# Second layer's attention: far score blocks made transposed by the matmul itself, four heads of a group per unit

## The reference, cut to what matters

```python
q = (x @ Wq.T) ... * hd ** -0.5        # 16 heads
k, v = ...                             # 4 groups, each repeated for 4 heads
scores = einsum('bhqd,bhkd->bhqk', q, k)
dist = clip(pos[None, :] - pos[:, None], -127, 127) + 127
bias = einsum('bhqd,kqd->bhqk', q, E[dist])
attn = softmax(scores + bias, axis=-1)
out = einsum('bhqk,bhkd->bhqd', attn, v) ... @ Wo.T
```

## Time and profile before

| | us |
|---|---|
| median of 3 runs | 1951.91 (1949.84 to 1952.54) |
| profiled execution, its own time | 1956.96 |
| its span in the trace | 1954.9 |

### The profile page before, as it was taken

How to read it: one execution, slowest core, us unless ns; L and a number is a source line. 1 busy time by engine, 2 the same in 40 slices (tenths; PEclk the granted TensorE clock), 3 DMA queues, 4 the chain that set the end, 5 groups by cost and what they waited for, 6 DMA issues and landing times. The chain is left out here.

```text
span 1954.9 us, 48846 instructions
## 1 busy us (share of the span) xinstructions
PE 1600.0 (82%) x17207; PEld 1157.0 (59%) x17207; DVE 1109.7 (57%) x3204; ACT 919.3 (47%) x1570; POOL 829.4 (42%) x1346
## 2 busy tenths in 40 slices
PE   3799999969999996326993269999995799999945
PEld 2466667655666664315762247777774577777733
DVE  5566666574666666560332756566566566565652
ACT  2355555444555553000321157777773466666622
POOL 2255555423555552024353025555552255555500
PEclk9899999989999998557997579999997799999968
DMA  3000000000000000421342025555550355555400
GB/s 116 1 1 0 0 0 0 1 1 1 1 0 0 0 0 1 167 94 56 76 94 39 5 92 183 179 177 179 180 172 1 115 180 179 179 176 180 152 1 22
DMA packets 102707, 146.63 MB, mean 75 GB/s; under 512 B 11632, under 2 KB 59120, under 8 KB 102640
## 3 DMA queue, kind: packets, MB, share of 16 engines
q1 hardware_dynamic: 95856, 140.87, 23.0%
q0 software_dynamic: 6784, 4.87, 1.9%
HBM read 68.49 MB, written 77.21 MB: 75 GB/s over the span
## 5 line engine op out<-in xcount | busy, mean ns | idle before, releaser
L496 ACT ACTIVATE t_Pt<-t_psT 128x512 f32<-128x512 f32 x1024 | 556.5, 595 | 471.2 <-PE t_psT L385 471.2
L468 POOL TENSOR_SCALAR t_Z<-t_Z,t_m 128x1024 f32<-128x1024 f32 x512 | 574.3, 1122 | 0.0
L385 PE MATMUL t_psT<-idf,t_Z 128*128 128x128 f32 x4096 | 562.2, 281 | 14.6 <-POOL t_Z L468 13.4
L385 PEld LDWEIGHTS t_psT<-idf,t_Z 128*128 128x128 f32 x4096 | 454.9, 145 | 100.7 <-ACT t_Pt L496 47.0
L439 DVE CUSTOM_DVE_ANT_0 t_Z<-t_psS,a1b_A 128x1024 f32<-128x1024 f32 x256 | 312.4, 1220 | 201.0 <-issue 201.0
L439 DVE CUSTOM_DVE_ANT_0 t_Z<-t_psS,a0b_L 128x1024 f32<-128x1024 f32 x256 | 312.3, 1220 | 190.0 <-issue 187.3
L360 PE MATMUL t_psO<-t_Pt,t_Vh 128*32 128x128 f32 x8192 | 329.9, 279 | 0.0
L467 POOL TENSOR_TENSOR t_touch<-t_m 128x1 f32<-128x1 f32 x512 | 98.7, 193 | 490.9 <-DVE t_m L439 488.9
L360 PEld LDWEIGHTS t_psO<-t_Pt,t_Vh 128*32 128x32 f32 x8192 | 192.4, 109 | 191.0 <-ACT t_Pt L496 158.1
L488 ACT ACTIVATE t_rows<-t_psE 128x512 f32<-128x512 f32 x256 | 152.9, 597 | 16.4 <-PE t_psE L346 15.3
L337 PE MATMUL t_psS<-a0b_KT,a0b_QT 72*128 (+1 forms) x512 | 154.7, 383 | 6.7 <-PEq L74 4.1
(11 more groups left out here) (233 smaller groups left out, 1444.5 us busy)
## 6 DMA issues: line engine op xcount, KB each, us to landing
relative_rows<-t_rows SPq DMA_DIRECT2D x256, 256.0 KB, 2.0
a1b_A<-relative_rows SPq DMA_DIRECT2D x192, 192.0 KB, 2.5
a1b_A<-relative_rows SPq DMA_DIRECT2D x64, 128.0 KB, 2.2
x_B<-in_b SPq DMA_DIRECT2D x1, 4096.0 KB, 18.1
x_A<-in_a SPq DMA_DIRECT2D x1, 4096.0 KB, 25.5
expert_rows<-zp SPq DMA_DIRECT2D x1, 2740.0 KB, 11.6
x_xe<-expert_rows SPq DMA_DIRECT2D x8, 342.5 KB, 3.1
x_WP<-in_moe_pre SPq DMA_DIRECT2D x8, 256.0 KB, 3.2
```

The source lines that it names most:

```text
L385: last = nc.tensor.transpose(psT[:, half, k * P:(k + 1) * P], Z[:, qt % 2, kt * P:(kt + 1) * P], idf[:])
L468: nc.gpsimd.tensor_scalar(Z[:, qt % 2, :], Z[:, qt % 2, :], -1.0, m[:, qt % 2:qt % 2 + 1], ALU.mult, ALU.add).then_inc(s_sub, 1)
L496: nc.scalar.activation(Pt[:, qt % 2, half * (N // 2):(half + 1) * (N // 2)], psT[:, half, :], ACT.Exp).then_inc(s_exp, 1)
```

## The change

The first layer keeps `attend`. The second layer uses a new function `attend_direct`, the clearing of A goes, and `project` scales the queries by plus instead of minus. The unit of work is now a group G: the four heads of one key/value group for one query tile; there are 32 groups per batch entry, all written out in code (no hardware loop). For each group and each key block kt one item of 128 keys x (4 heads x 128 queries) is made in a psT slot (a ring of three), exponentiated and multiplied with V:

- Scores with queries on the partitions are still made for all keys (`scores`, in chunks of 512 keys in a ring of three PSUM banks), but DVE writes out only the band (sum with A into Zb, with its maximum) and takes a plain `reduce_max` over the rest; `group_max` joins the parts.
- POOL subtracts the maximum from the band (four instructions of up to 384 elements) and splits the negated maximum into three bf16 parts (six small instructions on 128 x 4).
- PE turns these parts (`turn_max`) to 12 rows, DVE copies them out of PSUM (`max_rows`), and SP moves them by three DMAs into rows 72 to 74 of QT, against three rows of ones in KT. With them one bf16 matmul of 75 rows by 512 columns makes the scores of a far item already transposed and less the maximum.
- Band items are transposed as before, four per item.
- `values` runs per item, one head in each column strip; the eight items of a group are summed in PSUM, so one `to_rows` and one copy and division serve four query tiles of four heads.

```diff
+def attend_direct(nc, tag, b, QT, KT, V, attn, con, segments, EBT, scratch):
...
+    def item(G, i):
+        return G * 9 + (i if i < 4 else i + 1)
...
+                def ring_free(n):
...
+                    before = n - RR
+                    G, pos = before // 9, before % 9
+                    if pos == 4:
+                        if G + 1 < GROUPS:
+                            pe.wait_ge(s_me, G + 2)
+                        if G % 4 == 1 and G > 4:
+                            pe.wait_ge(s_div, G // 4)
+                    else:
+                        pe.wait_ge(s_exp, G * 8 + (pos if pos < 4 else pos - 1) + 1)
...
+                def unit(G, i):
...
+                    if kt in band(qt):
+                        if i == 0:
+                            pe.wait_ge(s_sub, (G + 1) * J)
+                        for j in range(J):
+                            last = nc.tensor.transpose(out[:, j * P:(j + 1) * P], Zb[...], idf[:])
+                    else:
+                        if kt == off(qt)[0]:
+                            pe.wait_ge(s_md[G % 2], 48 * (G // 2 + 1))
+                        var = 1 if kt * P < lo(qt) else 2
+                        last = nc.tensor.matmul(out, KT[0:KM, var * GKV + hq, kt * P:(kt + 1) * P],
+                                                QT[0:KM, hq * J:(hq + 1) * J, qt * P:(qt + 1) * P], start=True, stop=True)
+                    last.then_inc(s_u, 1)
...
+                for G in range(-3, GROUPS):          # PE
+                    for i in range(QT_N):
+                        if G >= 0:
+                            unit(G, i)
+                        if i < 2:
+                            if G >= 1:
+                                values(G - 1, i + 6)
+                        elif i == 2:
+                            if G >= 0 and (G == 0 or G % GRP):
+                                values(G, 0)
+                        elif i == 3:
+                            if G >= 0:
+                                if G and G % GRP == 0:
+                                    values(G, 0)
+                                values(G, 1)
+                        elif G >= 0:
+                            values(G, i - 2)
+                        if 0 <= G + 2 < GROUPS:
+                            scores(G + 2, i // 2, i % 2)
+                        if i % 2 and G + 3 < GROUPS:
+                            relative(G + 3, i // 2)
+                        if i == 3 and G >= 0:
+                            n = G * 9 + 4
+                            ring_free(n)
+                            if G + 1 < GROUPS:
+                                turn_max(G + 1, n)
+                            if G % 4 == 1 and G > 4:
+                                to_rows(G // 4 - 1, n)
...
+                for G in range(-2, GROUPS):          # DVE
+                    for j in range(J):
+                        if G + 2 < GROUPS:
+                            tile(G + 2, j)
+                            if j == J - 1:
+                                group_max(G + 2)
+                        if j == 0 and G > 0 and G % GRP == 0:
+                            copy_out(G // GRP - 1)
+                        if j == 2:
+                            if 0 <= G and G + 1 < GROUPS:
+                                max_rows(G + 1)
+                            if G % 4 == 1 and G > 4:
+                                divide(G // 4 - 1, G * 9 + 4)
...
+                            if i % 2 and G + 3 < GROUPS:      # ACT, after the exponential of item i
+                                gather(G + 3, i // 2)
...
+                def max_rows(G):                     # SP
+                    hq, qt = G // QT_N, G % QT_N
+                    sp.wait_ge(s_me, G + 1)
+                    for s in range(SPLIT):
+                        sp.dma_start(QT[KR + s:KR + s + 1, hq * J:(hq + 1) * J, qt * P:(qt + 1) * P], mr[s * J:(s + 1) * J, G % 2, :]).then_inc(s_md[G % 2], 16)
+
+                for G in range(-3, GROUPS):          # SP
+                    for j in range(J):
+                        u = (G + 3) * J + j
+                        if u < TILES:
+                            store(u)
+                        if 2 <= u < TILES + 2:
+                            fetch(u - 2)
+                        if j == 3 and 0 <= G + 1 < GROUPS:
+                            max_rows(G + 1)
...
-                    @block.vector
-                    def _(dve):
-                        nc.vector.memset(A[:], 0.0).then_inc(s_zero, 1)
-                        dve.wait_ge(s_zero, 1)
-
-                project(nc, f"p1{b}", b, xn, w, GKV, QT, KT, V, idf, idb, efar=ef)
-                attend(nc, f"t1{b}", b, QT, KT, GKV, V, A, y, con, segments, rel=(EBT, scratch))
+                project(nc, f"p1{b}", b, xn, w, GKV, QT, KT, V, idf, idb, efar=ef, scale=SCORE_SCALE)
+                attend_direct(nc, f"t1{b}", b, QT, KT, V, y, con, segments, EBT, scratch)
```

More of the change, by code:

```diff
@@ L26 @@
 BAND = 512
+GKV = 4
 RANK_ROWS = 32 * 64
@@ L124, in split, with project @@
             own(nc.vector.tensor_tensor(f, f, parts[:, i], ALU.subtract))
-def project(nc, tag, b, xn, w, gkv, QT, KT, V, idf, idb, pre=None, efar=None):
+def project(nc, tag, b, xn, w, gkv, QT, KT, V, idf, idb, pre=None, efar=None, scale=-SCORE_SCALE):
     nvar = 3 if efar is not None else 1
@@ L219, in _ @@
                         dve.wait_ge(s_qkv, n + 1)
-                        own(nc.vector.tensor_scalar(f[:, s, 0:wide], psQ[:, s, 0:wide], -SCORE_SCALE, None, ALU.mult))
+                        own(nc.vector.tensor_scalar(f[:, s, 0:wide], psQ[:, s, 0:wide], scale, None, ALU.mult))
                         if efar is not None:
@@ L1042, in sandwich @@
     place, placei, again = sb("place", [P, 1 + E]), sb("placei", [P, 1 + E], U32), sb("again", [P, E, NT])
-    con = {"idf": idf, "blk": blk, "below": below, "ones": ones, "j": cf[:, 0:1], "jfac": cf[:, 1:3],
+    fold4 = sb("fold4", [P, 4 * (DH + 1)])
+    con = {"idf": idf, "fold4": fold4, "idb": idb, "blk": blk, "below": below, "ones": ones, "j": cf[:, 0:1], "jfac": cf[:, 1:3],
            "rev": cf[:, 3:3 + E], "sel16": cf[:, 3 + E:3 + 2 * E],
@@ L1053, in sandwich @@
     with phase(nc, "load") as ph:
-        s_x, s_c, s_id = ph.sem("x"), ph.sem("c"), ph.sem("id")
+        s_x, s_c, s_id, s_fold = ph.sem("x"), ph.sem("c"), ph.sem("id"), ph.sem("fold")
         with nc.Block() as block:
@@ L1062, in _ @@
                 sp.wait_ge(s_x, 48)
+            @block.vector
+            def _(dve):
+                v = nc.vector
+                v.memset(fold4[:], 0.0).then_inc(s_fold, 1)
+                dve.wait_ge(s_fold, 1)
+                dve.wait_ge(s_x, 48)
+                for j in range(4):
+                    v.tensor_copy(fold4[32 * j:32 * j + 32, j * (DH + 1):(j + 1) * (DH + 1)], con["fold"][32 * j:32 * j + 32, :]).then_inc(s_fold, 1)
+                dve.wait_ge(s_fold, 5)
             @block.gpsimd
@@ L1160, in sandwich @@
         layer_norm(nc, "m1", y, add_to=X)
-    GKV = far.shape[1] // (2 * DH)
     with phase(nc, "a1") as ph:
@@ L1216, in sandwich @@
                 V = pb_.sb("V", [P, QT_N, GKV, DH + 1])
-                A = pb_.sb("A", [P, QT_N, N])
-                s_one, s_zero = pb_.sem("one"), pb_.sem("zero")
+                s_one = pb_.sem("one")
                 with nc.Block() as block:
```

213 lines of the change are left out of this document (added).

## The result

| | before | after |
|---|---|---|
| median, us | 1951.74 (1949.84 to 1952.54) | 2262.32 (2255.12 to 2264.71) |
| profiled execution, its own time | 1956.96 | 2264.71 |

Slower by 15.9%: the ratio is 1.1587 (95% interval 1.1559 to 1.1615). I forecast slower, 2050, range 1960 to 2120: the sign was right, the size was not. The profiled execution is 308 us longer, against a forecast of 100.

What follows compares the result with a forecast made beforehand. PE bounds the kernel before; after, a loop of PE's work and two waits takes 11.75 us per group against 9.84. Stage +56.7, twice +113, less 13.8 for clearing, plus 1: about +100, so 2050 us, range 1960 to 2120.

Steps and rivals of the forecast that it cites:

- PE's stream: PE's own work per group in the second layer's attention, without waits: 9.53 us, 7.74 with the lower bounds.
- values block of eight instructions: On PE, values of one item: 0.39 us, or 0.48 with the delay behind a bf16 matmul; bounds 0.29 and 0.58.
- late start: On PE, each block behind a bf16 matmul starts 0.10 us late.
- far item: On PE, one matmul of 512 columns 0.22, values 0.48, scores 0.22: 0.92 us.
- clearing A: Clearing of A, 6.9 us each on the path, goes: 13.8 us saved.
- Wait A: PE's first far item waits for the maximum rows' DMAs until 4.81 us after the last relative; stands 0.6, or 1.85.
- Wait B: PE's item 6 waits for DVE's max_rows to free the psT slot of turn_max: stands 1.14 us, bounds 0.7 and 1.5.
- POOL's chain: POOL's four band subtractions at 0.42 and six small instructions at 0.19: 2.9 us per group, under PE's 9.53.
- C: PE's turn_max waiting for POOL's parts of the maximum; not listed in the prediction, found in the trace after.
- rival 2: The clock falls besides, as PE stands 1.7 to 3 us per group: +81 us, 2131; chance 0.10.
- Rival 1: PE's stream stays the bound, the waits hidden: group 9.53 us, kernel 1924; chance 0.13.

Runs made afterwards that it cites:

- e8: Changed kernel with three reorderings: parts of the maximum first on POOL, their DMAs before the last store on SP, DVE's copy-out before tile(G+2, 2); 1931.7 us, 0.991 of before.
- e9: e8 with SP's order of the changed kernel put back, so only the wait for the maximum rows' DMAs is left; 2114.7 us, 1.077 of before.
- e5: Changed kernel with DVE making the negated maximum and POOL adding it instead of subtracting the maximum; 2188.1 us, 1.120 of before.
- e6: Changed kernel with POOL's six small instructions for the parts of the maximum ahead of its four subtractions; 2172.1 us, 1.113 of before.
- B alone: e8 with DVE's order of the changed kernel put back, so only item 6's wait for the maximum rows' copy is left; 2073.9 us.

## Why the prediction was wrong in size

**PE's stream: right within 3%.** 9.53 forecast, 9.30 at the full clock in e8. That the mean of e8's first entry is 9.52 is chance, since it holds 34 us at the half clock. The values block of eight instructions was 0.36 (I took 0.39), the late start 0.09 (0.10), a far item 0.90 to 0.91 (0.92): each term came out a little under. That the change saves next to nothing of PE's time, and that clearing A is a gain, stands.

**Wait A: right as a mechanism; in size by two errors that cancel.** The timeline on PE and SP, kernel after, at full clock:

```profile
1584.19 0.38 PE L593 MATMUL t_psE<-a_EBT,a1b_QT 72*128 72x512 bf16 x1
...
1586.07 1.84 SPq L870 DMA_DIRECT2D a1b_QT<-t_mr  x3
...
1589.06 0.38 PE L641 MATMUL t_psT<-a1b_QT,a1b_KT 75*128 75x512 bf16 x1 [1.14 <-DMA a1b_QT<-t_mr]
```

4.87 from the last relative to the far item; the sum said 4.81. SP's pitch was 0.6 and not 0.47, and the rows landed sooner than the 2.0 that I took. PE stood 1.14 here and not 0.6, since its own work in between was 3.73 and not 4.23 (this is one of the last groups, with fewer relatives). Nine groups of this kernel with three band items wait for the rows at the full clock: 4.85 to 4.89 in eight of them and 5.01 in one, with 0.9 of standing in five; in e9 it goes up to 5.9.

**Wait B: right as a mechanism, a third too long.** PE stood 0.77 in the group shown, not 1.14. From the start of the last chunk's matmul to item 6 it was 1.37 (1313.97 to 1315.34), not 1.57; the copy of the rows takes 0.21 and not 0.29.

**Step that failed, one: POOL's chain, left out of the waits.** "POOL: 1.12 per 1024 elements gives 0.42 per band of 352, four of them and six small ones of 0.19 are 2.9", and so "under that". It took 1244 and 923 ns, the six small ones 1.5 with the time between them: 6.4. And I asked only whether POOL was busy less than PE, not who waits for its last instruction; `turn_max` was not in my list of waits. The loop through it is, by the estimate above, 12.77 at full clock against my 11.75: 1.0 per group. e5 and e6, which take C away in two ways, give 1.2 each, a part of it again by the clock.

**Step that failed, two: the clock, taken as 1.00.** The sum ran at 1.00, and rival 2 had a chance of 0.10, "the clock was 1.00 in this stage". But that row was of a PE that never stood. The measured 14.72 is 2.0 over the 12.77 of full clock; and with C away, where my own list of waits was complete, 13.5 is 1.8 over my 11.75. So the mechanism of rival 2 was what happened, at more than its price of 1.4. It is the larger of the two: of the 3.0 us per group over the forecast, a third is POOL and two thirds the clock, by the estimate of 12.77. PE's own time says it more strongly: it stood 1.8 us per group in all, under the 2.2 that I had put down, and was busy 13.0 instead of 9.5, because the same matmuls ran slower. Over 62 periods the 3.0 us are 184 of the 208 us that the profiled execution lies above the forecast; the rest I have not taken apart.

**Rival 1** (1924 if the waits are hidden) described the kernel without its three waits: 1931.7 and 1928.9.

**The second entry of e8.** Its period is 9.93 against 9.52. It holds 66 us at the half clock, the first entry 34. 48 of the 66 begin behind one wait: PE stood 1.34 us ahead of values, for DVE's copy of the sums, and then ran on without a gap at 0.50. The timeline on PE and the stretch, e8_three:

```profile
1764.66 0.67 PE L656 MATMUL t_psO<-t_Pt,t_Vh 128*32 128x128 f32 x12 [1.34 <-DVE t_Os L755]
```

```profile
1765.00:1812.00 47.00, 47.00 (x303) 20.21 (x295) 19.18 (x85) 19.88 (x34) 18.24 (x31) 0.50 0.35 113
```

**What stays open.** No run fills all three waits of the kernel after, so whether filling alone would keep the clock is not shown. Nor is it shown why the clock stays low for 10 us behind one wait and for 61 behind another.

## What to carry to other kernels

For every instruction that an engine issues to be waited for, follow the loop it lies in, also where the engine is idle half of its time; three changes of order on three queues moved this kernel from 16% slower to 1% faster without taking an instruction away. Price a wait of PE not by its length alone: where PE was never idle before, the full clock in its rows tells nothing of a loop with one short stand per group, and the price was 2.3 to 5 times the stand, over half of it paid behind the wait, while PE was busy at the half clock. A busy share hides this (95% in e9): compare the busy time per unit of work. Such waits are to be taken away together: alone the three changes of order brought 7, 64 and 90 us, together 331.

## What the runs showed of the hardware

- POOL's `tensor_scalar` costs by its operation. Times 1 plus a column: 586 ns for 384 elements, 478 for 256, so 0.84 ns per element and 0.26 us fixed; by that 1024 elements are 1.12, the row of before, which was times -1 plus a column. Minus a column: 1244 and 923, 2.5 ns per element. Times 1 minus a column: 1572 and 1144, 3.3 ns per element. These are 1, 3 and 4 times 0.84. The Trainium skill ("GPSIMD Engine Reference", section 3.1) has 769 ns measured for 512 elements as the best case of a tight loop; by the lines above it would be 0.69 us with the addition, under that, and 1.57 us with the subtraction, twice it.
- With 0.6 us of waiting per group (A alone, 1.4 us at a time) the granted clock between 1200 and 1400 us was 0.69, with 0.8 (B alone) 0.78, without both 1.00: the sum of the waiting alone doesn't order them.
- A busy PE doesn't bring the full clock back at once: behind single waits of 1.67 us (e9) and 1.34 us (e8) it ran at 0.50 for 61 and 47 us, busy 60.8 and 47.0 of them.
- Three DMAs of 1 KB from SBUF into SBUF are issued in 1.82 to 1.84 us, 0.6 each, where the earlier trace rows have 0.47; behind the last of them the waiting matmul started 1.15 us after the issue's end (1587.91 to 1589.06).
